# Halved ACT copies between exponentials, paired row maxima, and the attention output normed through DRAM and GpSimd

## What is computed

```
for i in range(6):
    q, k, v = split(adaln(x) @ qkv_w.T);  q, k = rope(q), rope(k)
    x = x + softmax(q k / 4) v @ so_w.T
    q = rope(adaln(x) @ cq_w.T);  k = rope(ctx @ ck_w.T);  v = ctx @ cv_w.T
    x = x + softmax(q k / 4) v @ co_w.T
    x = x + gelu(adaln(x) @ f1_w.T + f1_b) @ f2_w.T + f2_b
```

## Time and profile before

| | us |
|---|---|
| median of 3 runs | 4453.81 (4446.65 to 4462.31) |
| profiled execution | 4442.28, span 4440.6 |
| PE busy | 3940.5 (89%) |
| DVE busy | 2907.1 (65%) |
| ACT busy | 2561.9 (58%) |
| POOL busy | 857.7 (19%) |

### The profile page before, as it was taken

One profiled execution on the slowest core, in us unless ns is written; L12 is line 12 of the kernel. 1 busy time (PEld: TensorE's weight loads), 2 busy tenths in 40 slices (PEclk: granted clock), 3 DMA queues, 4 the chain that ended last, 5 costly groups with the idle time before them and its releaser, 6 DMA issues. The chain is left out here.

```text
span 4440.6 us, 68492 instructions
## 1 busy us (share of the span) xinstructions
PE 3940.5 (89%) x20630; PEld 1833.7 (41%) x20630; DVE 2907.1 (65%) x4711; ACT 2561.9 (58%) x4302; POOL 857.7 (19%) x518
## 2 busy tenths in 40 slices
PE   3699999999999999999999999999999999997467
PEld 1233344533344533345433345433345433354355
DVE  3777766677766678766678766678766677752311
ACT  1376656667666567666567665567666566654122
POOL 4312121112121112211111211111211121200133
PEclk7799999999999999999999999999999999999689
DMA  5354323244323244332244332244332344410234
GB/s 162 85 135 108 97 69 78 63 108 120 87 78 72 60 113 119 87 80 65 67 108 116 94 72 66 68 108 116 97 75 59 74 129 111 109 30 13 83 99 95
DMA packets 271578, 396.39 MB, mean 89 GB/s; under 512 B 28312, under 2 KB 218400, under 8 KB 270880
## 3 DMA queue, kind: packets, MB, share of 16 engines
q1 hardware_dynamic: 263904, 382.18, 34.1%
q0 software_dynamic: 7296, 9.51, 1.3%
HBM read 226.63 MB, written 170.67 MB: 89 GB/s over the span
## 5 line engine op out<-in xcount | busy, mean ns | idle before, releaser
L837 ACT ACTIVATE prob<-ps 128x512 f32<-128x512 f32 x3072 | 1768.2, 596 | 1225.2 <-PE ps L761 1207.6
L999 DVE TENSOR_REDUCE negmax<-ps 128x2 f32<-128x1024 f32 x1536 | 1836.7, 1219 | 217.6 <-PE ps L788 195.2
L761 PE MATMUL ps<-qstack,kstack 114*128 114x512 bf16 x3072 | 1162.4, 389 | 100.1 <-ACT prob L837 84.8
L774 PE MATMUL psv<-prob,v 128*32 128x512 f32 x6144 | 829.5, 612 | 0.0
L761 PEld LDWEIGHTS ps<-qstack,kstack 114*128 114x128 bf16 x3072 | 284.6, 97 | 1190.3 <-ACT prob L837 794.5
L616 POOL TENSOR_TENSOR rot<-ropep 128x512 f32<-128x512 f32 x96 | 122.5, 1276 | 2486.7 <-DVE ropep L1032 2467.7
L788 PE MATMUL ps<-kstack,qstack 49*128 49x512 bf16 x3072 | 496.8, 388 | 97.9 <-DVE negmax L999 76.8
L736 PE MATMUL side<-anat,wf 128*128 128x256 f32 x1536 | 377.1, 388 | 9.9 <-DVE hT L1037 8.9
L1037 DVE TENSOR_SCALAR hT<-side,f1b 128x256 f32<-128x256 f32 x384 | 168.2, 479 | 303.6 <-PE side L736 303.6
L747 PE MATMUL side<-wf,hT 128*128 128x256 f32 x1536 | 347.9, 379 | 2.8 <-DVE x L1044 1.6
L736 PEld LDWEIGHTS side<-anat,wf 128*128 128x128 f32 x1536 | 285.6, 192 | 65.7 <-DVE hT L1037 30.9
(11 more groups left out here) (158 smaller groups left out, 3722.1 us busy)
## 6 DMA issues: line engine op xcount, KB each, us to landing
bounce<-parts SPq DMA_DIRECT2D x480, 256.0 KB, 2.5
qstack<-bounce SPq DMA_DIRECT2D x384, 192.0 KB, 5.5
kstack<-bounce SPq DMA_DIRECT2D x384, 192.0 KB, 6.1
bounce<-low SPq DMA_DIRECT2D x96, 256.0 KB, 2.1
ctxT<-in_ctxT SPq DMA_DIRECT2D x24, 512.0 KB, 3.9
nw<-in_nwT SPq DMA_DIRECT2D x18, 512.0 KB, 11.3
w<-in_w SPq DMA_DIRECT2D x16, 512.0 KB, 4.8
wself<-in_wself SPq DMA_DIRECT2D x24, 256.0 KB, 4.0
```

The source lines that it names most:

```text
L761: nc.tensor.matmul(ps2[:, n % RING2, :], kk[0:ROWS, h, kt * P:(kt + 1) * P], q[0:ROWS, h, :], start=True, stop=True).then_inc(s_p2full, 1)
L774: mm = nc.tensor.matmul(psv[32 * i:32 * i + 32, 0, :], v[j % 2][:, kt, (HD + 1) * h:(HD + 1) * h + 32], prob[:, 4 * (u % 2) + i, :], start ...
L837: nc.scalar.activation(prob[:, 4 * (u % 2) + i, :], ps2[:, n % RING2, :], ACT.Exp, scale=HD ** -0.5).then_inc(s_prob, 1)
L999: nc.vector.tensor_reduce(out_at, ps1[:, 2 * (n % 2):2 * (n % 2) + 2, :], AX, ALU.max, negate=True).then_inc(s_p1free, 1)
```

## The change

1. `osum` is written to DRAM (`value_sums`), each group of four heads by one DMA (`write_sums`). `load_attention` loads the 16 rows of sums as a tile of 128x64 (`den`), the numerators straight into the layout of `aT`, waits for one reciprocal on DVE at place 4 (`RECIP_PLACE`), writes it to DRAM and loads it spread over 128 partitions (`recips`, which shares its buffer with `nT`). POOL multiplies (128x1024), and O follows. T1 and T2 are gone from PE, DVE and ACT.
2. `hi` and `mid` are two instructions of 128x512, one behind each exponential of the place.
3. Where the even place of a unit holds a chunk that DVE reads, DVE does both maxima of the unit in front of it.
4. The places are dealt anew. In short slots HQ and HK go to odd places, O from 19, 21 to 18, 20, the last two copies one place later. In long slots all moves forward by one to three places, the second GELU from 27 to 25.
5. The experts' transposes run two parts ahead instead of one.

```diff
 SHORT_PLACES = {
-    "HV": [1, 3], "T1": [2, 4, 5, 7], "HT": [6, 8], "HQ": [9, 10], "HK": [12, 14],
-    "T2": [15, 17], "O": [19, 21],
+    "HV": [1, 3], "HT": [6, 8], "HQ": [9, 11], "HK": [13, 15], "O": [18, 20],
 }
 LONG_PLACES = {
-    "HV": [1, 3], "T1": [2, 4, 5, 7], "HT": [6, 8], "T2": [9, 10], "O": [11, 12], "HQ": [13, 14],
-    "HK": [15, 16], "LT": [17, 18], "F1": [19, 20, 21, 22, 23, 24, 25, 26], "F2": [27, 28, 30, 31],
+    "HV": [1, 3], "HT": [5, 7], "O": [8, 10], "HQ": [9, 11], "HK": [12, 13], "LT": [15, 16],
+    "F1": [17, 18, 19, 20, 21, 22, 23, 24], "F2": [26, 27, 29, 30],
 }
-    "LT": dict(stats=[12, 12, 12, 12], aggregate=13, newton=15, tiles=[15, 15, 16, 16]),
+    "LT": dict(stats=[10, 10, 10, 10], aggregate=11, newton=13, tiles=[13, 13, 14, 14]),
-SHORT_SPLIT = (13, 15, 18, 20)
-LONG_SPLIT = (16, 18, 20, 22)
-GELU_PLACES = (23, 27)
+RECIP_PLACE = 4
+SHORT_SPLIT = (13, 15, 19, 21)
+LONG_SPLIT = (13, 15, 17, 19)
+GELU_PLACES = (21, 25)
...
+            def write_sums(j, g):
+                sp.wait_ge(s_os, place.jobs(j, 4) + g + 1)
+                sp.dma_start(sums[j % 2][4 * g:4 * g + 4].rearrange("h r n -> (h r) n"), osum[:, g, :]).then_inc(s_sums, 16)
+            def load_attention(j):
+                sp.wait_ge(s_sums, place.jobs(j + 1, 64))
+                sp.dma_start(den[:, :], sums[j % 2][:, HD].rearrange("h (c n) -> h c n", c=P // H)).then_inc(s_den, 16)
+                for k in range(KD):
+                    sp.dma_start(aT[:, k, :], sums[j % 2][8 * k:8 * k + 8, 0:HD]).then_inc(s_aload, 16)
+                sp.wait_ge(s_recip, place.jobs(j + 1, 1))
+                sp.dma_start(inverse[j % 2].rearrange("h (c n) -> (h c) n", c=P // H), recip[:, :]).then_inc(s_inv, 16)
+                sp.wait_ge(s_inv, place.jobs(j + 1, 16))
+                for k in range(KD):
+                    sp.dma_start(recips[:, k, :], inverse[j % 2][8 * k:8 * k + 8, None, :].to_broadcast([8, HD, S])).then_inc(s_aload, 16)
...
+                if tail:
+                    sp.wait_ge(s_full, side_done)
+                    write_sums(k - 2, 3)
+                    load_attention(k - 2)
...
                 if p2:
                     shift_rows(k, k - 1, 1)
+                    write_sums(k - 1, 0)
...
                 if head:
                     write_and_load(k + 1)
+                if p2:
+                    write_sums(k - 1, 1)
+                    write_sums(k - 1, 2)
                 if p1:
                     shift_rows(k, k, 0)
...
+                if tail:
+                    pool.wait_ge(s_aload, place.jobs(k - 1, 64))
+                    nc.gpsimd.tensor_tensor(aT[:, :, :], aT[:, :, :], recips[:, :, :], ALU.mult).then_inc(s_anorm, 1)
...
                     if p2:
                         exp(k - 1, u, 2 * half)
+                    if splits_here:
+                        (hi, mid)[split_step](k + 1, w, 0)
+                    if p2:
                         exp(k - 1, u, 2 * half + 1)
+                    if splits_here:
+                        (hi, mid)[split_step](k + 1, w, 1)
...
-                    if p1:
+                    both = any(what in ("HQ", "HK", "O", "F1", "F2") for what, c in plan[2 * u])
+                    if p1 and half == 0:
                         maximum(k, at)
+                        if both:
+                            maximum(k, at + 1)
+                    if p1 and half == 1 and not both:
+                        maximum(k, at)
...
+                    if tail and at == RECIP_PLACE:
+                        dve.wait_ge(s_den, place.jobs(k - 1, 16))
+                        nc.vector.reciprocal(recip[:, :], den[:, :]).then_inc(s_recip, 1)
```

More of the change, by code:

```diff
@@ L335, in layers @@
         mrow = sb("mrow", [16, 2, S], BF16)
-        recip = sb("recip", [P, TT, H])
+        den = sb("den", [P, H * S // P])
+        recip = sb("recip", [P, H * S // P])
         st = sb("st", [P, TT, 6])
@@ L342, in layers @@
         fence_at = sb("fence_at", [P, 1])
+        sums = [nc.dram_tensor(f"value_sums{i}", (H, 32, S), F32, kind="Internal").ap() for i in range(2)]
+        inverse = [nc.dram_tensor(f"inverse{i}", (H, S), F32, kind="Internal").ap() for i in range(2)]
         bounce = [nc.dram_tensor(f"bounce{i}", (NPROD, D, S), BF16, kind="Internal").ap() for i in range(2)]
@@ L498, in write_part @@
                         sp.wait_ge(s_second[hf], place.jobs(j, SECOND_DMAS))
-                sp.wait_ge((s_hi, s_mid, s_low)[part], place.jobs(j, 2) + w + 1)
+                if part < 2:
+                    sp.wait_ge((s_hi, s_mid)[part], place.jobs(j, 4) + 2 * w + 2)
+                else:
+                    sp.wait_ge(s_low, place.jobs(j, 2) + w + 1)
                 for r in range(NPROD):
@@ L612, in split @@
                 if j or w:
-                    pool.wait_ge(s_mid, done)
+                    pool.wait_ge(s_mid, place.jobs(j, 4) + 2 * w)
                     pool.wait_ge(s_low, done)
@@ L681, in side_work @@
             def side_work(k, what, c):
-                if what == "T1":
+                if what == "O":
                     if c == 0:
-                        pe.wait_ge(s_os, place.jobs(k - 1, 4))
-                    transposes(begin(k, what, c), [osum[:, g, c * P:(c + 1) * P] for g in range(4)])
-                elif what == "T2":
-                    if c == 0:
-                        wait_read(pe, place, k, "T1", 2)
-                        wait_read(pe, place, k, "T1", 3)
-                    transposes(begin(k, what, c), [anat[:, t, c * P:(c + 1) * P] for t in range(TT)])
-                elif what == "O":
-                    if c == 0:
-                        wait_read(pe, place, k, "T2", 0)
-                        wait_read(pe, place, k, "T2", 1)
+                        pe.wait_ge(s_anorm, place.jobs(k - 1, 1))
                     w = wcross if is_cross(k - 2) else wself
@@ L840, in copy_group @@
             def copy_group(k, j, g):
-                if g == 0 and k >= 2:
-                    wait_filled(act, place, k, "T1", 3)
+                if j > 0:
+                    act.wait_ge(s_sums, place.jobs(j - 1, 64) + 16 * (g + 1))
                 act.wait_ge(s_pv, place.jobs(j, 16) + 4 * g + 4)
@@ L887, in side_work @@
                     modulate(k, what, c)
-                elif what == "T2":
-                    wait_filled(act, place, k, what, c)
-                    nc.scalar.activation(aT[:, c, :], bank, ACT.Copy).then_inc(s_read, 1)
                 elif what == "HV":
@@ L909, in head0 @@
                     modulate(-1, "HT", c)
-                hi(0, 0)
-                mid(0, 0)
-                hi(0, 1)
-                mid(0, 1)
+                for w in range(2):
+                    for step in (hi, mid):
+                        for i in range(2):
+                            step(0, w, i)
             def slot(k, p2, p1, tail, head):
@@ L1010, in side_work @@
             def side_work(k, what, c):
-                if what not in ("T1", "HQ", "HK", "O", "F1", "F2"):
+                if what not in ("HQ", "HK", "O", "F1", "F2"):
                     return
```

71 lines of the change are left out of this document (38 added, 33 removed).

## The result

| | before | changed |
|---|---|---|
| median of the runs, us | 4454.35 (4446.65 to 4462.31) | 4718.67 (4709.45 to 4729.40) |
| profiled execution, span | 4440.6 | 4718.8 |
| PE busy, whole span | 3940.5 (89%) | 3963.3 (84%) |
| mean granted clock, whole span | 0.962 | 0.922 |

The ratio is 1.0594, 95% interval 1.0565 to 1.0624. The sign was forecast; the size (264 us instead of 91) lies outside the range.

The account below looks back on a forecast made before the run. PE was taken as the bound. From 4442.3 us, -110 - 3 + 132 + 22 + 40 - 18 + 25 + 3 gave 4533, with 11.5 for the median 4545; forecast 4490 to 4600 (0.60), range 4440 to 4650.

Parts of the forecast that it names:

- Part 6: O in long slots waits for the chain of inverses and POOL's product: 1.8 us in 22 slots, +40 us.
- Part 4: Reciprocal's wait for `den` at place 4: 5.3 us behind short slots, +132 us; 1.1 behind long ones, +22 us.
- Parts 1 and 2: Short slots, transposes gone and waits gone: 4.6 us less each, -110 us; slots 0 and 1 another -3 us.
- Part 2: Short slots' waits for maxima and rope gone, half of those for exponentials: 2.7 us gained, less 0.28 for even places.
- Part 5: Row maxima land 3.1 us behind the next slot's start, moving some 3 of the 5.3 us there; not added.
- the clock's term: PE standing 3 to 5 us loses full clock at times: 1.0 us for 25 slots, +25 us (0 to 85).
- The first rival: The queue doesn't hold the sums back, so no wait at pair 7 in unit 3: 4366 us, chance 0.17.
- Part 3: Long slots: 1.9 us from transposes gone, against 1.9 for the second GELU and 0.3 for places: 0 (-44 to +44).
- Part 7: The rest: experts -18 us (-20 to -5), clock +25 (0 to 85), last two slots +3 (-4 to +15).
- O waiting 4 us and a clock term of 60: The heavier rival: O's wait +48 us, clock falling longer in 25 slots +60 us: 4653 us, chance 0.16.

Follow-up runs that it names:

- e1: The changed kernel with the last F2 chunk of a long slot at place 31 instead of 30: 4673.5 us, 1.0500 of the kernel before.
- e8: The kernel before with the halves, the short slots' new HQ, HK and T2 places and the experts' edit, without DMA chain or pairs: 4362.8 us, ratio 0.9803.
- e4: The changed kernel with the inverses written twice, so that each spread load reads 16 rows instead of 8: 4699.5 us, 1.0550 of the kernel before.
- e10: The changed kernel with F2's last chunk at 31 and O reading another, ready tile in long slots: 4527.9 us, 1.0175 of the kernel before.
- e15: The changed kernel with single maxima in the old order in long slots: 4687.6 us, 1.0531 of the kernel before.
- e14: The changed kernel with old places and single maxima in long slots, row maxima ahead of two sums writes, inverses written twice: 4429.4 us, 0.9932 of the kernel before.
- e7: The kernel before with both maxima of a unit ahead of DVE's work on its even-place chunk: 4513.5 us, ratio 1.0147.
- e2b: The changed kernel with long slots at the old places, ACT's copies of sums waiting for all four earlier writes: 4509.6 us, 1.0136 of the kernel before.
- e5: The kernel before with the experts' edit alone, reads of gathered rows two parts ahead: 4428.4 us, ratio 0.9947.

## Why the prediction was right in sign and wrong in size

The steps that failed are two terms for long slots. Part 6 put O's wait for the chain at 1.8 us a slot, 40 us in all, where it was 3.9 us, and 4.8 with e1's edit, and cost 146 us with the clock behind it. Part 4 took the end of the stack loads behind long slots from the kernel before, although the change moves the F2 chunk that had covered them (45 us). The pairs in long slots had no term (31 us), and the clock had 25 us where it took at least 92.

**Parts 1 and 2 (short slots -4.6 us): right.** From unit 1 to unit 8 and from 10 to 14, where no new wait stands, the median short slot went down by 4.6 us; unit 9, with O, up by 0.5. What Part 2 gave as its cause was half wrong: e8 gets rid of most of the same waits without the pairs (1.2 to 0.2 for maxima, 2.2 to 1.2 for exponentials; 0.3 of the rope's 0.4 stays), so they go with the places, HQ and HK at odd ones.

**Part 4, behind short slots (+5.3), with Part 5 (3.1 of it at the slot's start): the sum came out, in part by luck.** The wait for the row maxima at the start, Part 5, is right: 3.4 us against 3.1. The main cost of Part 4, the reciprocal's wait, is not there: the part of it that was to stay in unit 3 is 2.2 us in the prediction, and PE's wait for maxima there is 0.6 us, 0.2 before the change. `den` lands at 10.1 us in the slot shown against the 15.1 that I had. Of these 5.0 us the delayed start is 4.1; the last stack load, issued 0.3 us ahead of that start instead of 5.1 behind it, comes another 1.3 sooner. What fills the gap in the sum is the clock behind the wait: units 15 and 0 together are 5.9 us longer (medians), some 3.4 of it the wait. Short slots behind short ones were to grow by 0.7 us, 1.7 with the clock's term, and grew by 2.0 (66.4 to 68.4); the five behind long ones were to shrink by some 3 us and shrank by 1.4, with `den`'s wait in unit 3. The first rival's sign, a wait in unit 3 under 2.9 us, is so met, but not for its reason: in long slots behind long ones, where the write of the last sums is issued right behind the stack loads, it lands 0.3 to 0.7 us behind the last of them. The queue does hold it back, as Part 4 has it.

**Part 4, behind long slots, and Part 3: a step that failed.** I took 7.7 us for the landing of the last stack load from the kernel before, and priced the long slots' moves by DVE, GELU and rope alone. I did not ask what F2's last chunk at place 31 covered. It was SP's head start: at place 30 the loads are issued at 5.5 us instead of 0.8, the reciprocal comes at 14.4 instead of 11, and HT, which I had given -0.6 us for its odd places, waits 3.76 us in the slot shown. The diff had it (31 to 30), but I followed SP's queue through the short slots alone. e1: 45 us. With F2 at 31, the reciprocal comes at 11.0 and PE is ready for O at 17.7, where the prediction had 10.9 for `den` and 17.6 for O.

**Part 6 (O +1.8 us): the mechanism was right, the term was mis-sized.** In e1 the write of the inverses takes 2145.76 - 2142.37 = 3.4 us until SP goes on (2.1 taken), the spread loads 4.9 until POOL starts (3.9), the product 2.34 (2.1): 10.7 us against 8.1, and O stands 4.65. The write is late because it stands behind 512 KB of numerators. The trace of the changed kernel shows this: issued less than 2 us behind their last load, it holds SP for 3.6 us (median of 24), issued 3.5 us or more behind it, as in the short slot shown (1882.17 to 1883.65), for 1.5 (median of 19). The 3.9 for the spread loads was that of a load over 128 rows. The Trainium skill, "DMA: Bandwidth & Descriptors", section "Why a DMA increments its semaphore by 16 and not by 1", says that a DMA uses the largest number of engines, up to 16, that divides the slowest dimension of both sides; the trace agrees, with a busy share of 0.50 for 8 rows and 1.01 for 16. The prediction's estimate from that rule was 1.9 us more a slot (22 x 1.9 is 42 us, not 43) and stood outside the sum; e4 measured 1.1 in its slot. With it the sum would have been nearer, and still short. e10 prices O's wait, clock included: 146 us, where +40 stood in the sum.

**The pairs in long slots** had no term at all. They are change 3, and I had counted them a gain in the part on short slots; 31 us in the changed kernel (e15), 37 at the old places (e14), 78 in the kernel before (e7, where T1 counts too). In the changed kernel they cost at HK, where PE waits 2.1 us a slot for the rope instead of 1.3. The other readings of Part 3 held: LT waits about the same (2.3 us, 2.5 before), and the second GELU's new wait is 1.7 us (1.9 taken).

**Part 7.** Experts: -18 predicted, -24 measured. Clock: +25 (0 to 85) predicted; at least 92 us, the PE busy time beyond what the same matmuls have in e14. It goes with the waits above; with a wait of 4 us the clock went to 0.50 for some 5 us, and I had taken 1.0 us a slot and none for O's wait. The last two slots: +3 (-4 to +15) predicted, +17 measured; no experiment looked at them.

**Sum for a long slot:** +2.9 us predicted behind a long one (1.1 and 1.8), +12.5 measured in these 16 (96.8 to 109.3); behind a short one +7.1 predicted (5.3 and 1.8), +9.6 measured in these six (97.8 to 107.4). In the mean of all 22 it is +11.7. e1 takes back 2.6, e10 6.2, single maxima 1.7: 10.5 of 11.7. The waits tell the same from the other side: PE waits 15.2 us in a long slot instead of 5.3, for POOL's product 3.9 (0 before), at HT 2.3 (0), for the row maxima 1.0 (0), for exponentials 3.4 (1.1), for the rope 2.1 (1.3). The rest is the clock, less what the transposes gave; these two were not measured apart. With O at its old places and single maxima (e14) a long slot is at 97.6, no shorter than before, though it has six transposing chunks fewer.

The range was too narrow for another reason too. Its upper end was built from O waiting 4 us and a clock term of 60; both came about, together with a wait (HT's) that I had excluded with a number from the kernel before.

## What to carry to other kernels

When a table of places moves, look at each entry that crosses the last instruction some queue waits for: one chunk, moved by one place, took away the cover of ten loads. Price a chain of DMAs through DRAM by its worst neighbours in the queue, not by the same bytes alone, and put its reader behind the end of that; with O three places later in long slots (e2b) PE waited 0.3 us a slot for the same chain. And try the parts of a change apart: here three of its parts (the halves, the short slots' places, the experts) are worth 2.0% without the chain and the pairs, and the one with the largest idea behind it gave nothing in any version tried (e14, the best with the chain, is at the time of e5, which has the experts' edit alone).

## What the runs showed of the hardware

- A wait of PE of 4 us was followed by about 5 us at half the clock: products of 0.39 us took 0.61, a group of 1.06 took 1.94. Over the slots of the changed kernel this came to at least 92 us (3612 us of PE busy time at 0.94 against 3520 at 0.97 in e14).
- Three DMA issues on ACT's queue kept ACT from its next exponential for 2.27 us, and PE for 2.56.
- The 512 KB spread of inverses reached POOL 5.6 us behind its issue when read as 8 rows, and 4.5 when read as 16; the busy share of the 16 DMA engines was 0.50 in the one and 1.01 in the other.
- A write of 32 KB held SP for 3.6 us when it was issued less than 2 us behind 512 KB of loads, and for 1.5 us when it was issued 3.5 us or more behind them.
